# Cross attention on one core: the mask transposed by DMAs instead of TensorE and VectorE, with a reordered third maximum and a reordered start

## What is computed

```python
Q = heads(x @ Wq.T + bq);  K = heads(ctx @ Wk.T + bk);  V = heads(ctx @ Wv.T + bv)
scores = Q @ K.T / sqrt(32)
scores = where(mask == 0, -1e9, scores)         # mask: 16 x 512 x 512 int32
y = (softmax(scores) @ V) @ Wo.T + bo + x
out = (y - mean(y)) / sqrt(var(y) + 1e-5) * ln_g + ln_b
```

## Time and profile before

| | us |
|---|---|
| median of 3 runs | 1756.46 (1754.41 to 1756.84) |
| the profiled execution | 1753.16 |
| its span in the trace | 1751.4 |
| PE busy in it | 1652.2 (94%) |
| ACT, POOL, DVE busy in it | 1342.4, 1284.4, 1155.7 |
| mean granted TensorE clock | 0.982 of full speed |

### The profile page before, as it was taken

One profiled execution on the slowest core, in us unless ns is written; L12 is line 12 of the kernel. 1 busy time (PEld: TensorE's weight loads), 2 busy tenths in 40 slices (PEclk: granted clock), 3 DMA queues, 4 the chain that ended last, 5 costly groups with the idle time before them and its releaser, 6 DMA issues.

```text
span 1751.4 us, 24771 instructions
## 1 busy us (share of the span) xinstructions
PE 1652.2 (94%) x7716; PEld 977.5 (56%) x7716; DVE 1155.7 (66%) x2835; ACT 1342.4 (77%) x1537; POOL 1284.4 (73%) x835
## 2 busy tenths in 40 slices
PE   3689999999999999999999999999999999999987
PEld 2456656565665656566565555656555565656532
DVE  4465676666667676666767667676766767676653
ACT  2078788887877878787787878778787878878774
POOL 3056577877877887787887787788778769778765
PEclk8799999999999999999999999999999999999998
DMA  9667577576766757766775866677586666656501
GB/s 335 181 170 215 156 208 197 185 201 196 207 184 198 210 171 206 205 194 179 203 213 161 226 193 198 174 215 206 156 231 188 197 187 202 206 156 193 165 19 66
DMA packets 181058, 330.65 MB, mean 189 GB/s; under 512 B 37440, under 2 KB 37440, under 8 KB 180928
## 3 DMA queue, kind: packets, MB, share of 16 engines
q1 hardware_dynamic: 180928, 329.08, 64.9%
HBM read 239.87 MB, written 89.13 MB: 188 GB/s over the span
## 4 chain that ended last, share of the span: by engine, by line
PE 81%; DVE 7%; issue 4%; ACT 3%; DMA 2%; POOL 2%; SPq 0%; DVEq 0%; POOLq 0%; ACTq 0%
PE proj_bank L913 43%; PE ring L811 11%; PE exp_banks L826 11%; PE ctx_bank L842 10%; PE ring L862 3%; DVE ring L650 3%; ACT qk_hi L550 2%; POOL total L422 1%; PE ring L871 1%; DVE proj_bank L667 1%; DMA stack_scratch<-qk_lo 1%; PE exp_banks L949 1%; DVE qk_lo L675 1%; POOL total L430 1%; DMA q_stack<-stack_scratch 0%
## 5 line engine op out<-in xcount | busy, mean ns | idle before, releaser
L650 DVE CUSTOM_DVE_ANT_0 ring<-ring,bias 128x512 f32<-128x512 f32 x1024 | 687.3, 712 | 320.7 <-PE ring L811 320.6
L530 ACT ACTIVATE probs<-exp_banks 128x1024 f32<-128x1024 f32 x512 | 523.7, 1023 | 282.1 <-PE exp_banks L826 282.0
L504 ACT CAST exp_banks<-biasT 128x1024 f32<-128x1024 bf16 x512 | 520.7, 1017 | 23.7 <-ACT probs L530 0.7
L826 PE MATMUL exp_banks<-q_stack,k_stack 98*128 98x512 f32 x1024 | 373.6, 447 | 5.4 <-ACT exp_banks L504 5.3
L811 PE MATMUL ring<-k_stack,q_stack 96*128 96x512 f32 x1024 | 331.6, 403 | 11.8 <-DVE maxes L650 8.3
L430 POOL TENSOR_TENSOR total<-total,probs 128x1024 f32<-128x1024 f32 x126 | 297.3, 2380 | 9.3 <-POOL total L422 0.4
L422 POOL TENSOR_TENSOR total<-total,probs 128x2048 f32<-128x2048 f32 x63 | 289.8, 4600 | 9.6 <-ACT probs L530 3.2
L422 POOL TENSOR_TENSOR total<-probs 128x2048 f32<-128x2048 f32 x63 | 290.4, 4609 | 0.1
L437 POOL CAST max_parts<-maxes 128x16 fp32r<-128x16 f32 x64 | 12.6, 196 | 370.5 <-DVE maxes L650 370.5
L842 PE MATMUL ctx_bank<-probs,v 128*32 128x512 f32 x2048 | 275.3, 610 | 0.7 <-DVE ctxT L708 0.7
L826 PEld LDWEIGHTS exp_banks<-q_stack,k_stack 98*128 98x128 f32 x1024 | 194.0, 191 | 110.0 <-issue 68.1
(11 more groups left out here) (77 smaller groups left out, 1861.0 us busy)
## 6 DMA issues: line engine op xcount, KB each, us to landing
w_tile<-w_scratch SPq DMA_DIRECT2D x126, 512.0 KB, 4.4
k_stack<-stack_scratch SPq DMA_DIRECT2D x192, 256.0 KB, 5.3
q_stack<-stack_scratch SPq DMA_DIRECT2D x192, 256.0 KB, 7.0
stack_scratch<-qk_hi SPq DMA_DIRECT2D x128, 256.0 KB, 2.1
stack_scratch<-qk_lo SPq DMA_DIRECT2D x128, 256.0 KB, 2.5
raw<-cT_dram SPq DMA_DIRECT2D x64, 256.0 KB, 4.9
raw<-xT_dram SPq DMA_DIRECT2D x64, 256.0 KB, 4.6
raw<-mask_dram SPq DMA_DIRECT2D x64, 256.0 KB, 4.4
```

The source lines that it names most:

```text
L504: nc.scalar.copy(exp_banks[:, 2 - 2 * wave:4 - 2 * wave, :], biasT[:, kc:kc + 1, :].to_broadcast([P, 2, L])).then_inc(seeded, 1)
L530: nc.scalar.activation(probs[:, u % PS, 2 - 2 * wave:4 - 2 * wave, :], exp_banks[:, 2 - 2 * wave:4 - 2 * wave, :], ACT.Exp).then_inc(exps, 1)
L650: nc.vector.tensor_tensor_reduce(out=ring[:, n % 2], in0=ring[:, n % 2], in1=bias[:, c], scale=1.0, scalar=LOWEST, op0=ALU.subtract, op1=A ...
L826: mm = nc.tensor.matmul(exp_banks[:, h], k_stack[0:3 * D + 2, at, kc * P:(kc + 1) * P], q_stack[0:3 * D + 2, at, :], start=False, stop=Tru ...
```

## The change

**The mask.** `turn_mask` goes from PE to SP. In the same units and in the same order SP issues four DMA transposes, each of a 128 x 128 block of bf16 from `bias` to `biasT`. The VectorE copy, the ring slots of the mask and the identity matrix are gone. `seed` waits for the four DMAs (`mask_turned[kc]`) and negates while it copies. The conversion of the next mask waits for the last of these DMAs in place of the last mask matmul.

**The third maximum.** In units with sums (y % 4 = 0), VectorE's third maximum now comes ahead of `finish_tile`. For an O tile it comes between the two additions: the first of them is a function of its own, `bias_output`. In other units it stays behind.

**The start.** GpSimd makes no identity. VectorE writes the rows of -1 first of all, and splits Wk and Wq ahead of the loop (Wk's low half goes to `q_stack` for a while, since `k_stack` has its rows of -1). Wv is split at y = -9. SP loads the last piece of x ahead of Wv and Wo, stores the split Wk at y = -13 and the split Wq at y = -10, and the first group's K stack and Q stack are issued at y = -9 around the load of weights. ScalarE loads its table by a copy of one column before anything has been loaded. PE writes the banks with 16 matmuls on the first weight tile in place of 4 on Wv.

```diff
@@ Plan
-                         self.mask(y), self.sums(y)):
+                         self.sums(y)):
@@ sync
+            load_raw(0, 1, NK - 1)
             load_weight(WvT, probs[:, 2], wv_loaded)
             load_weight(WoT, wo[:, :, :], wo_loaded)
...
-            load_raw(0, 1, NK - 1)
...
+            def turn_mask(s, kc):
+                sp.wait_ge(bias_ready, (s + 1) * NC)
+                if s >= 1:
+                    sp.wait_ge(seeded, 2 * (s * UPS - NC + kc) + 2)
+                for c in range(NC):
+                    sp.dma_start_transpose(biasT[:, kc, c * P:(c + 1) * P],
+                                           bias[:, c, kc * P:(kc + 1) * P]).then_inc(
+                                               mask_turned[kc], FULL)
...
-                if PLAN.stack_group(y) is not None:
+                if y == -13:
+                    scratch(0, (ctxT[:, 0:NG], q_stack[:, 2 * HG:3 * HG].bitcast(FP32)), wk_split,
+                            wk_scratch)
+                if y == -10:
+                    scratch(1, (total[:, :, :], rows[:, :, :]), wq_split, wq_scratch)
+                if y == -9:
+                    stack("K", 0)
+                if PLAN.stack_group(y):
                     stack("K", PLAN.stack_group(y))
                     stack("Q", PLAN.stack_group(y))
...
-                if y == -10:
-                    scratch(0, (ctxT[:, 0:NG], k_stack[:, 2 * HG:3 * HG].bitcast(FP32)), wk_split,
-                            wk_scratch)
+                tile = PLAN.tile(y + 2)
+                if y < -7 and tile and tile[0] in "QK":
+                    load_weights(tile)
                 tile = PLAN.tile(y - 1)
                 if tile and tile[0] in "QK":
                     keep_halves(tile)
                 if y == -9:
-                    scratch(1, (total[:, :, :], rows[:, :, :]), wq_split, wq_scratch)
...
+                    stack("Q", 0)
...
+                if PLAN.mask(y):
+                    turn_mask(*PLAN.mask(y)[1:])
                 for tile in PLAN.rows_due(y - 1, PLAN.SCALED):
                     store_row(tile)
@@ scalar
             def seed(u, wave):
...
-                    act.wait_ge(ring_free, PLAN.ring["M", s, kc] + 1)
+                    act.wait_ge(mask_turned[kc], FULL * NC * (s + 1))
...
-                nc.scalar.copy(exp_banks[:, 2 - 2 * wave:4 - 2 * wave, :],
-                               biasT[:, kc:kc + 1, :].to_broadcast([P, 2, L])).then_inc(seeded, 1)
+                nc.scalar.activation(exp_banks[:, 2 - 2 * wave:4 - 2 * wave, :],
+                                     biasT[:, kc:kc + 1, :].to_broadcast([P, 2, L]),
+                                     ACT.Copy, scale=-1.0).then_inc(seeded, 1)
...
+            nc.scalar.copy(warm[:, :], eps_t[:, :]).then_inc(table_loaded, 1)
@@ vector
+            nc.vector.memset(k_stack[3 * D:3 * D + 2, :, :].bitcast(FP32),
+                             -1.0).then_inc(minus_ones, 1)
             dve.wait_ge(wk_loaded, FULL)
             first_tile(0, wk_raw[:, :, 0])
+            split(wk_raw, by_tile(ctxT[:, 0:NG]), by_tile(q_stack[:, 2 * HG:3 * HG]), wk_split)
...
             first_tile(1, wq_raw[:, :, 0])
...
-            split(wk_raw, by_tile(ctxT[:, 0:NG]), by_tile(k_stack[:, 2 * HG:3 * HG]), wk_split)
+            dve.wait_ge(consts_made, 4)
+            split(wq_raw, by_tile(total[:, :, :]), by_tile(rows[:, :, :]), wq_split)
...
-            def copy_mask(s, kc):
-                n = PLAN.ring["M", s, kc]
-                dve.wait_ge(ring_filled, n + 1)
-                if s >= 1:
-                    dve.wait_ge(seeded, 2 * (s * UPS - NC + kc) + 2)
-                nc.vector.tensor_copy(biasT[:, kc], ring[:, n % 2]).then_inc(ring_free, 1)
...
                 tile = PLAN.tile(y - 1)
+                ring_wanted = PLAN.sums(y)
+                if tile and tile[0] == "O":
+                    bias_output(tile)
+                if ring_wanted:
+                    row_max(y, 2)
                 if tile:
                     finish_tile(tile)
-                row_max(y, 2)
+                if not ring_wanted:
+                    row_max(y, 2)
                 row_max(y, 3)
-                if PLAN.mask(y):
-                    copy_mask(*PLAN.mask(y)[1:])
@@ tensor
+            pe.wait_ge(first_hi, 1)
+            for b in range(4 * HG):
+                mm = nc.tensor.matmul(exp_banks[:, b % HG], w_tile[:, 0, 0, 0],
+                                      w_tile[:, 0, 0].rearrange("p t c -> p (t c)"),
+                                      start=True, stop=True)
+            mm.then_inc(banks_written, 1)
...
-                for c in range(NC):
-                    mm = nc.tensor.matmul(ring[:, n % 2, c * P:(c + 1) * P],
-                                          bias[:, c, kc * P:(kc + 1) * P], ident_bf[:, :],
-                                          start=True, stop=True)
-                mm.then_inc(ring_filled, 1)
```

More of the change, by code:

```diff
@@ L159, in xattn_program @@
         recipT = sb("recipT", [P, NK, P])
-        ident_bf = sb("ident_bf", [P, P], BF16)
         ones = sb("ones", [P, D])
@@ L210, in xattn_program @@
         tail_done, tail_biased = sem("tail_done"), sem("tail_biased")
+        mask_turned = [sem(f"mask_turned{n}") for n in range(NC)]
         mask_scaled, o_biased = sem("mask_scaled"), sem("o_biased")
@@ L349, in _ @@
                 if y == -9:
-                    scratch(1, (total[:, :, :], rows[:, :, :]), wq_split, wq_scratch)
[L351 to L357, removed]
+                    stack("Q", 0)
+                tile = PLAN.tile(y + 2)
+                if y >= -7 and tile and tile[0] in "QK":
+                    load_weights(tile)
+                tile = PLAN.tile(y + 4)
+                if tile and tile[0] == "O":
+                    load_row(tile)
                 seq, at = y // UPS + 1, y % UPS
@@ L514, in convert_mask @@
                     act.wait_ge(ring_free, PLAN.ring["A", s * NG - 1, c, HG - 1] + 1)
-                    act.wait_ge(ring_filled, PLAN.ring["M", s - 1, NC - 1] + 1)
+                    act.wait_ge(mask_turned[NC - 1], FULL * NC * s)
                 nc.scalar.activation(bias[:, c], words, ACT.Relu, bias=masked_t[:, 0:1],
@@ L614, in _ @@
             first_tile(1, wq_raw[:, :, 0])
-            dve.wait_ge(qk_bias_loaded, 2 * FULL)
-            nc.vector.tensor_scalar(bq_s[:, :], bq_s[:, :], SCALE, None,
-                                    ALU.mult).then_inc(bq_scaled, 1)
-            split(wk_raw, by_tile(ctxT[:, 0:NG]), by_tile(k_stack[:, 2 * HG:3 * HG]), wk_split)
+            dve.wait_ge(consts_made, 4)
+            split(wq_raw, by_tile(total[:, :, :]), by_tile(rows[:, :, :]), wq_split)
             def prologue(y):
[L621 to L624, removed]
+                if y == -9:
                     dve.wait_ge(wv_loaded, FULL)
                     split(probs[:, 2], wv_hi[:, :, :], wv_lo[:, :, :], wv_split)
+                if y == -8:
                     dve.wait_ge(consts_loaded, 4 * FULL)
@@ L629, in prologue @@
                         [P, NG, P])).then_inc(bv_wide, 1)
[L630 to L633, removed]
                 if y == -3:
@@ L660, in turn_max, with bias_output @@
                     "p a h c -> p (a h c)").bitcast(FP32)).then_inc(max_turned, 1)
+            def bias_output(tile):
+                m = PLAN.o[tile]
+                dve.wait_ge(proj_done, PLAN.no[tile] + 1)
+                nc.vector.tensor_tensor(proj_bank[:, 0], proj_bank[:, 0], bo_all[:, :],
+                                        ALU.add).then_inc(o_biased, 1)
             def finish_tile(tile):
@@ L781, in _ @@
         def _(pe):
-            pe.wait_ge(consts_made, 7)
-            def prologue(y):
[L785 to L788, removed]
-                                              start=True, stop=True)
-                    mm.then_inc(banks_written, 1)
+            pe.wait_ge(consts_made, 4)
+            pe.wait_ge(first_hi, 1)
[4 more added lines that the diff above has]
+            mm.then_inc(banks_written, 1)
+            def prologue(y):
                 if y == -5:
@@ L932, in _ @@
                     context(y - 1)
-                if PLAN.mask(y):
-                    turn_mask(*PLAN.mask(y)[1:])
                 if PLAN.sums(y) and PLAN.sums(y)[1] < LAST:
```

26 lines of the change are left out of this document (6 added, 20 removed).

## The result

The changed kernel takes 1832.97 us (median of 4 runs, 1828.36 to 1836.96) against 1755.44 of the kernel before on the same chip: ratio 1.044, 95% interval [1.041, 1.047]. It is slower by 77.5 us where the sum gave 48 us less (1705).

A forecast was written before the change was run, and what follows sets the result against it. PE, busy 94% of the span, was taken as the bound. Loop 40.2 us less plus start 13.8 less, minus 6 for transposes, made 48 less than the median: 1705 us, forecast 1690 to 1715, range with rivals A and B 1690 to 1746.

The forecast's parts named there:

- The third maximum: VectorE's third maximum in units with sums: moved earlier, it frees the bank sooner and removes all 15.9 us of waiting.
- The start: Before the loop: transfers, a memset, mask blocks and clock give 3 + 4.8 + 4 + 2 = 13.8 us less.
- the sum: Whole kernel: 40.2 us less in the loop, 13.8 less at the start, 6 more for transposes: 48 us less, 1705.
- Unit 14: A loop unit that loses its mask block on PE: from 6.00 us to 5.83.
- Unit 1: A loop unit that loses its mask block on PE: from 6.45 us to about 5.85.
- Unit 4: A loop unit with sums beside an O tile: from 7.90 us to 7.55, with no wait of the sums for DVE.
- ACT's 5 us: ScalarE's `seed` as ACTIVATE in place of CAST: 512 x 0.01 us more, covered by ACT's idle time, counted as 0.
- 256 DMA transposes on SP: Mask blocks on SP's queue: four issue in 1.7 us; block kc = 3 takes 3.8 against 3.4, costing 6 us.
- SP needs over 1 us to issue one transpose, so that stacks come late: One of the signs, on SP's queue, that the prediction named as proving it wrong; no time or chance given.
- B: Rival at block kc = 3: four transposes run one after another at 1.4 us each, 5.6 in all; 1734 us; chance 0.20.
- C: Rival, slower: block kc = 3 becomes every sequence's wait, each us over 3.4 costing 16; up to 1777 us; chance 0.14.
- A: Rival: the start stays transfer-bound (3, not 13.8) and half the sums' 15.9 us returns at another wait; 1724 us; chance 0.18.

## Why the prediction was wrong

**The steps that held.** Unit 14 fell back to 5.82 us on the mean, as forecast (5.83). Unit 1 did so only in the kernel with one transpose a block (5.82). Unit 13 stayed at 6.0 in the change and 6.3 in that kernel, against 5.85. Unit 4 went to 7.35 (forecast 7.55), and the sums no longer wait for DVE. The third maximum gave 20.0 us against 15.9: moved alone, it took 0.55, 0.55 and 0.60 off units 4, 8 and 12, and 0.5 came back in unit 13. The first exp came 11.1 us earlier in the change and 11.8 in the kernel with one transpose a block, against 13.8. ACT's 5 us cost nothing that shows: PE waits for its seed 3.4 us in all, 5.3 before.

**The step that failed** is the term "256 DMA transposes on SP", in its first number. I took a plain DMA's 0.43 us as the issue time, since the trace before has no transposing one, and it is 1.23. Eight in a row took 10.05, which is (10.05 - 1.23) / 7 = 1.26 from one to the next: 5 us a block in place of 1.7. I bounded the landing from both sides, 1.4 to 7.0, and the issue not at all. With one value for it, the three other blocks were put down as free ("about two units until `seed` reads them"). At 5 us a block they are not free, neither to what stands behind them on the queue nor to their own reader: SP reached blocks kc = 1 and 2 so late that ACT waited for both, 69 us in all. The prediction names the stack as the next work on SP, and then gives it no time. The working needed was this: three blocks make the stack 15.9 - 5.1 = 10.8 us later. Before, the Q stack's last DMA had some 6 us to spare (an estimate: issued by 915.1, 7.0 us to land, and unit 2 at 928.34). So some 5 us of the delay reach unit 2, where the gap is 4.31, and block kc = 3 comes behind that stack. The prediction names as its own refutation "SP needs over 1 us to issue one transpose, so that stacks come late"; this is what came, and it had no rival and no chance of its own.

**The size of the loss.** The kernel with one transpose a block and the changed kernel differ in span by 1826.1 - 1699.5 = 126.6 us. PE's busy time is 1680.4 - 1629.2 = 51.2 us longer for the same 7472 matmuls, which goes with the lower clock behind the gaps (mean granted clock 0.953 against 0.985); the other 75.4 are idle time of PE. Who counts only gaps misses two fifths of the loss. By unit, unit 2 takes 12.5 us on the mean against 6.2 and unit 1 takes 7.65 against 5.82; over 16 sequences these two make up the loss.

**The rivals.** B had the pace nearly right (1.4 us each, it was 1.26) and priced it only at block kc = 3, so it came to 1734. By the Trainium skill, "VectorE: DVE Perf Modes", The three transpose paths, a 128 x 128 transpose takes 1309 ns by DMA; this case's pace of 1.26 us is near. The preference for TensorE, which stands on the same page under "Rules for kernel authors", holds here for 16 such blocks a sequence (1726 against 1833). The rule speaks of 128 x 128 alone; for blocks of 128x512, where the same 1.23 us turns four of them, the runs show the opposite (1702 against 1726). C was right in its kind, ACT waiting up to 6.9 us for `biasT` in every sequence, and its landing like a queued stack came too (up to 8.4 us). What it lacked was why: the queue was not near empty there, since the block went out late and the stack stood just ahead of it. Of A's kind the 0.5 us came that unit 13 took back, and the start gave 2 to 3 us less than its 13.8.

**The sum itself.** With a hold near the one that it assumed, 1.7 us a block, the forecast was good: 1705 against 1708.0 with plain copies (2.46 us a block) and 1701.5 with one transpose a block (1.2). Some of that is luck: the third maximum gave 4 us more than its term, and the start 2 to 3 less.

## What to carry to other kernels

Price a DMA by three numbers, each bounded from both sides: how long it holds the queue that issues it, how long until it lands with what is ahead of it, and what stands behind it on the queue. The reader of its data may have two units of slack while the next instruction of the queue has none. Where the hold is per instruction, change the layout so that one instruction moves what four did, before moving the instructions about.

## What was not expected of the hardware

- A transposing DMA from SBUF to SBUF held SP for 1.23 us (median) for 32 KB and 128 KB alike, and four of 64 KB took 5.08 together. Plain copies of 32 KB held it for 0.60, against 0.43 for the 256 KB loads. The Trainium skill, "Advanced Engine Details and Errata", X-Bar Transpose (TRN2), has transposing DMAs as fast as regular ones. For the landing in an empty queue this is near (2.3 us at best against 1.8 of the plain copies of 32 KB); for the issuing queue it is not, at twice the time.
- DMAs of one queue that follow six of 256 KB landed late with these: four transposes 7.6 to 10.5 us after issue, against 2.4 with nothing large ahead of them.
- The gap of 4.31 us on PE was followed by 5 us at a granted clock of 0.53.

Left open: why the hold is the same for all three sizes, and whether ACT's queue would be held as long; neither was tried. Nor was another place for the block kc = 3 with one transpose a block, where 5.3 us of ACT's waits are left.
